# Token lists built by TensorE in SBUF instead of by scatters in DRAM: an attention and mixture-of-experts layer on one core

## What is computed

```python
logits = xt @ gate_w.T
_, idx = top_k(logits + beta, 2)
c = zeros((B, E)).at[arange(B)[:, None], idx].add(sigmoid(logits[idx]))
combined = einsum('beh,be->bh', expert_outputs(xt), c)
shared_out = (silu(xt @ sg) * (xt @ su)) @ sd
return x + attention(xn) + combined + shared_out
```

## Time and profile before

| | us |
|---|---|
| median of 3 runs | 1900.78 (1877.45 to 1905.29) |
| the profiled execution | 1892.56 |
| its span, first to last instruction | 1890.8 |
| mean granted TensorE clock in it | 0.92 |
| PE / DVE / ACT / POOL busy | 89% / 60% / 51% / 51% |
| stage p | 0 to about 330 |
| between p and the first expert matmul | 330 to 348.8 |
| stage c | to about 1050 |
| stage b | to the end |

### The profile page before, as it was taken

One profiled execution on the slowest core, in us unless ns is written; L12 is line 12 of the kernel. 1 busy time (PEld: TensorE's weight loads), 2 busy tenths in 40 slices (PEclk: granted clock), 3 DMA queues, 4 the chain that ended last, 5 costly groups with the idle time before them and its releaser, 6 DMA issues.

```text
span 1890.8 us, 39124 instructions
## 1 busy us (share of the span) xinstructions
PE 1679.5 (89%) x11313; PEld 1347.0 (71%) x11313; DVE 1134.2 (60%) x3793; ACT 963.7 (51%) x1914; POOL 962.1 (51%) x915
## 2 busy tenths in 40 slices
PE   5787776699999999999999789999989999899987
PEld 4565654588888888888888556666666666666666
DVE  5657664466566566666665656666656666556642
ACT  4333432445445445445454355666656665556653
POOL 1434345322221221221220268888888888888886
PEclk9778777799999999999999679999989998889998
DMA  5546645544444444444455367666666666566642
GB/s 180 184 162 222 226 173 201 174 152 153 144 146 153 143 153 147 146 155 148 147 150 118 83 140 160 157 158 158 154 144 134 157 153 143 127 152 151 152 116 74
DMA packets 219824, 287.89 MB, mean 152 GB/s; under 512 B 67193, under 2 KB 133882, under 8 KB 219642
## 3 DMA queue, kind: packets, MB, share of 16 engines
q1 hardware_dynamic: 177226, 210.71, 39.9%
q0 software_dynamic: 17728, 38.30, 8.3%
q10 hardware_dynamic: 24816, 38.28, 5.6%
HBM read 194.92 MB, written 82.31 MB: 147 GB/s over the span
## 4 chain that ended last, share of the span: by engine, by line
PE 56%; issue 11%; POOL 8%; DMA 7%; DVE 6%; ACT 5%; another core or an unknown queue 4%; SPq 2%; ACTq 1%; DVEq 0%; POOLq 0%
PE psum L149 30%; PE psum L757 12%; PE psum L1225 4%; PE psum L1265 3%; DMA plain_arena<-y_d,b_ix 3%; POOL plain_arena L1174 2%; DMA split_arena<-k_d 2%; PE psum L1248 2%; PE psum L849 2%; POOL plain_arena L1149 2%; POOL split_arena L1166 1%; DVE plain_arena L1471 1%; POOL plain_arena L1147 1%; ACT plain_arena L1368 1%
## 5 line engine op out<-in xcount | busy, mean ns | idle before, releaser
L149 PE MATMUL psum<-split_arena 128*128 128x512 f32 (+2 forms) x4560 | 1026.5, 378 | 21.3 <-POOL split_arena L1166 8.5
L149 PEld LDWEIGHTS psum<-split_arena 128*128 128x128 f32 x4560 | 794.9, 202 | 179.3 <-issue 19.1
L1471 DVE CUSTOM_DVE_ANT_0 plain_arena<-psum,mask 128x256 f32<-128x256 f32 (+1 forms) x1024 | 340.0, 386 | 275.5 <-PE psum L1225 265.6
L831 POOL DMA_INDIRECT plain_arena<-xn_d,c_ix x156 | 152.4, 977 | 526.0 <-PE psum L849 479.5
L1368 ACT ACTIVATE plain_arena<-psum 128x512 f32<-128x512 f32 (+1 forms) x512 | 251.3, 543 | 278.4 <-PE psum L1248 249.4
L757 PE MATMUL psum<-split_arena 128*128 128x256 f32 x1872 | 233.8, 285 | 0.0
L757 PEld LDWEIGHTS psum<-split_arena 128*128 128x128 f32 x1872 | 226.9, 192 | 0.1
L360 POOL DMA_INDIRECT order_d<-plain_arena,slot x128 | 124.4, 972 | 198.2 <-DVE slot L618 161.1
L1225 PE MATMUL psum<-split_arena 48*128 48x256 f32 (+1 forms) x1024 | 166.6, 350 | 62.6 <-DMA split_arena<-k_d 32.0
L895 ACT ACTIVATE plain_arena<-psum 128x512 f32<-128x512 f32 x156 | 93.4, 599 | 218.0 <-PE psum L149 211.3
L1225 PEld LDWEIGHTS psum<-split_arena 48*128 48x128 f32 x1024 | 104.1, 201 | 139.6 <-issue 67.9
(11 more groups left out here) (146 smaller groups left out, 1745.1 us busy)
## 6 DMA issues: line engine op xcount, KB each, us to landing
plain_arena<-in_gate_w SPq DMA_DIRECT2D x39, 512.0 KB
plain_arena<-in_up_w SPq DMA_DIRECT2D x39, 512.0 KB
plain_arena<-in_down_w SPq DMA_DIRECT2D x39, 512.0 KB
y_d<-plain_arena ACTq DMA_DIRECT2D x39, 512.0 KB, 2.6
plain_arena<-in_x SPq DMA_DIRECT2D x32, 512.0 KB
q_d<-split_arena SPq DMA_DIRECT2D x32, 512.0 KB
k_d<-split_arena SPq DMA_DIRECT2D x32, 512.0 KB
split_arena<-q_d SPq DMA_DIRECT2D x128, 128.0 KB, 4.0
```

The source lines that it names most:

```text
L149: last = pe.matmul(out, lhs_t(p), rhs(q), start=(begins and c == 0 and k == 0), stop=(ends and c == len(chunks) - 1 and k == 2), skip_grou ...
L831: pool.indirect_dma_start(c_x[:, a, :], None, xn_d, bass.IndirectOffsetOnAxis(c_ix[:, u, a, 0:1], 0)).then_inc(c_ldx, 16)
L1471: last = dve.tensor_tensor_reduce(b_junk[:, 2 * par + i % 2, 0:cols], psum[:, par, at:at + cols], mask[:, 2 * P - cols:2 * P], -1.0, 3e38, ...
```

## The change

The list in DRAM, its blanking, the 128 scatters, the 40 list loads and `c_ix` go. In their place stands a table in SBUF, `order[p, n]`: the row number that belongs to slot 128n + p, for NC = 156 columns. It is a sum over all (row, choice) pairs of an outer product: a row vector that marks partition `slot mod 128`, times a column vector that marks column `slot div 128` and holds the row number.

- POOL, for each batch (2T = 8 pairs of tile and choice): 6 small instructions in a chain that split slot into mod and div, then 24 `tensor_scalar` instructions that write bf16 marks: `in_row` (128 columns), and `in_col` twice (156 columns: the multiple of 128 of the row number, and its remainder).
- PE, at the end of each turn, `tokens_to_slots` of t-2: 16 bf16 matmuls (128 x 128 weights, 156 columns), summed in PSUM bank 1.
- DVE, at the end of each turn, `token_places` of t-2: adds the 156 columns to `order_f`. After the turns one copy to `order`.
- PE's `turn_rows` also waits for `token_places` of an earlier turn (`p_or`), and the value totals move from bank 1 to bank 6.
- POOL's gathers in stage c take their indices from `order`, and wait for no list load; SP's loop in stage c no longer waits for the gather nor loads lists.
- In a block, slot a*128+p now stands at partition p, tile a, so `y_d` is stored in runs of 1 KB in place of 4 KB.

```diff
-            pool.memset(blank, 0).then_inc(s_norow, 1)
+            pool.memset(order_f[:, :], 0.0).then_inc(s_oz, 1)
...
             for b in range(B):
+                v = b % 2
+                flat = slot[:, b * T:(b + 1) * T, :].rearrange("p t k -> p (t k)")
                 pool.wait_ge(p_at, b + 1)
-                for a in range(T):
-                    for c in range(2):
-                        pool.indirect_dma_start(
-                            order_d, bass.IndirectOffsetOnAxis(slot[:, b * T + a, c:c + 1], 0),
-                            token[:, b * T + a, :], None).then_inc(p_sc, 16)
+                if b >= 2:
+                    pool.wait_ge(p_om, b - 1)
+                then = chain(b)
+                then(pool.tensor_copy(slot_at[:, :], flat))
+                then(pool.tensor_scalar(slot_pc[:, 1, :], slot_at[:, :], 1.0 / P, 0.5 * (1 - P) / P, ALU.mult, ALU.add))
+                then(pool.tensor_scalar(slot_pc[:, 1, :], slot_pc[:, 1, :], ROUND, None, ALU.add))
+                then(pool.tensor_scalar(slot_pc[:, 1, :], slot_pc[:, 1, :], -ROUND, None, ALU.add))
+                then(pool.tensor_scalar(slot_pc[:, 0, :], slot_pc[:, 1, :], -float(P), None, ALU.mult))
+                then(pool.tensor_tensor(slot_pc[:, 0, :], slot_pc[:, 0, :], slot_at[:, :], ALU.add))
+                for n in range(2 * T):
+                    pool.tensor_scalar(in_row[:, v, n, :], steps_f[:, 0:P], slot_pc[:, 0, n:n + 1], None, ALU.is_equal)
+                    pool.tensor_scalar(in_col[:, v, 0, n, :], steps_f[:, :], slot_pc[:, 1, n:n + 1],
+                                       float(P * (b * T + n // 2)), ALU.is_equal, ALU.mult)
+                    last = pool.tensor_scalar(in_col[:, v, 1, n, :], steps_f[:, :], slot_pc[:, 1, n:n + 1],
+                                              column[:, 0:1], ALU.is_equal, ALU.mult)
+                last.then_inc(p_oh, 1)
...
                 after(pe, p_rd, b - 2)
+                after(pe, p_or, b - 3)
...
+            def tokens_to_slots(b, v):
+                pe.wait_ge(p_oh, b + 1)
+                after(pe, p_or, b)
+                for n in range(2 * T):
+                    for k in range(2):
+                        last = pe.matmul(psum[:, 1, 0:NC], in_row[:, v, n, :], in_col[:, v, k, n, :],
+                                         start=(n == 0 and k == 0), stop=(n == 2 * T - 1 and k == 1))
+                last.then_inc(p_om, 1)
...
+                if old_b is not None:
+                    tokens_to_slots(old_b, old_u % 2)
...
+            def token_places(b):
+                dve.wait_ge(p_om, b + 1)
+                dve.tensor_tensor(order_f[:, :], psum[:, 1, 0:NC], order_f[:, :], ALU.add).then_inc(p_or, 1)
...
                     allot(done[0])
+                if old[0] is not None:
+                    token_places(old[0])
             dve.sem_inc(p_lo, 2 * KD)
             over_turns(dve, turn)
 
+            dve.wait_ge(p_or, B)
+            dve.tensor_copy(order[:, :], order_f[:, :]).then_inc(p_ord, 1)
...
             weights(0, None)
-            sp.wait_ge(p_sc, 32 * T * B)
-            for u in range(2):
-                order(u, u)
             projected(sp)
...
-                sp.wait_ge(c_ldx, 16 * T * blk + 16 * T)
-                order(blk + 2, u)
...
                 for a in range(T):
-                    pool.indirect_dma_start(c_x[:, a, :], None, xn_d, bass.IndirectOffsetOnAxis(c_ix[:, u, a, 0:1], 0)
+                    pool.indirect_dma_start(c_x[:, a, :], None, xn_d,
+                                            bass.IndirectOffsetOnAxis(order[:, T * blk + a:T * blk + a + 1], 0)
                                             ).then_inc(c_ldx, 16)
...
-                act.dma_start(y_d[ds(blk * BLK, BLK), :].rearrange("(p a) d -> p a d", p=P),
+                act.dma_start(y_d[ds(blk * BLK, BLK), :].rearrange("(a p) d -> p a d", p=P),
```

More of the change, by code:

```diff
@@ L352, in p_gpsimd, with chain, then @@
                                channel_multiplier=1).then_inc(s_const, 1)
-            pool.wait_ge(s_blank, 16)
-            pool.wait_ge(s_iota, 3)
+            pool.wait_ge(s_steps, 1)
+            ROUND = 12582912.0
+            def chain(b):
+                k = [0]
+                def then(ins):
+                    k[0] += 1
+                    ins.then_inc(p_ps, 1)
+                    pool.wait_ge(p_ps, 6 * b + k[0])
+                return then
             for b in range(B):
+                v = b % 2
+                flat = slot[:, b * T:(b + 1) * T, :].rearrange("p t k -> p (t k)")
                 pool.wait_ge(p_at, b + 1)
-                for a in range(T):
-                    for c in range(2):
-                        pool.indirect_dma_start(
-                            order_d, bass.IndirectOffsetOnAxis(slot[:, b * T + a, c:c + 1], 0),
-                            token[:, b * T + a, :], None).then_inc(p_sc, 16)
+                if b >= 2:
[14 more added lines that the diff above has]
+                last.then_inc(p_oh, 1)
         def p_tensor(pe):
@@ L428, in turn @@
                         prefix(done_b)
+                if old_b is not None:
+                    tokens_to_slots(old_b, old_u % 2)
             pe.wait_ge(s_const, 7)
             over_turns(pe, turn)
+            pe.wait_ge(p_vb, T * B)
             for m in range(KD):
                 for c in range(KD):
-                    last = pe.matmul(psum[:, 1, m * B:(m + 1) * B], wvg_raw[:, c, m * P:(m + 1) * P], xsum[:, c, :],
+                    last = pe.matmul(psum[:, 6, m * B:(m + 1) * B], wvg_raw[:, c, m * P:(m + 1) * P], xsum[:, c, :],
                                      start=(c == 0), stop=(c == KD - 1))
@@ L696, in p_vector @@
             for m in range(KD):
[L697 removed]
+                dve.tensor_scalar(vtot[:, :, m], psum[:, 6, m * B:(m + 1) * B], bv_col[:, m:m + 1], ATTN_EPS,
                                   ALU.add, ALU.mult)
@@ L728, in moe_attention_layer @@
         c_ldx = sem("c_rows_gathered")
-        c_il = [sem(f"c_order_loaded{u}") for u in range(2)]
-        c_ix = sb("c_ix", [P, 2, T, 16], U32)
         c_tr = sem("c_transposed")
@@ L826, in c_gpsimd, with gather @@
         def c_gpsimd(pool):
-            def gather(blk, u, n):
-                after(pool, c_tr, blk)
-                hold(pool, c_il[u], 16 * n + 16)
+            def gather(blk):
+                if blk:
+                    pool.wait_ge(c_tr, blk)
                 for a in range(T):
-                    pool.indirect_dma_start(c_x[:, a, :], None, xn_d, bass.IndirectOffsetOnAxis(c_ix[:, u, a, 0:1], 0)
+                    pool.indirect_dma_start(c_x[:, a, :], None, xn_d,
+                                            bass.IndirectOffsetOnAxis(order[:, T * blk + a:T * blk + a + 1], 0)
                                             ).then_inc(c_ldx, 16)
@@ L835, in c_gpsimd @@
                 pool.wait_ge(p_xst[v], 16 * (B // 2))
-            gather(0, 0, 0)
+            pool.wait_ge(p_ord, 1)
+            gather(0)
             pool.wait_ge(s_proj, 4)
             pool.memset(b_k.bitcast(F32), 1.0).then_inc(b_kz, 1)
-            def body(blk, u, n, more):
-                if more:
-                    gather(blk + 1, 1 - u, n + u)
-            over_blocks(pool, body)
+            for blk in range(1, NBLK):
+                gather(blk)
         def c_tensor(pe):
```

37 lines of the change are left out of this document (21 added, 16 removed).

## The result

The changed kernel took 1954.78 us (median of 4 runs, 1941.44 to 1962.14) where the kernel before took 1894.09 (4 runs): a ratio of 1.032 with a 95% interval of 1.024 to 1.040, slower. The forecast was 1856, and 1905 the end of the range. The profiled execution took 1949.99, its span is 1948.2 us.

What follows compares the result with a forecast made beforehand. Stage p was taken as held by scatters delaying PE's signals, stage c by PE. Turns -36, p to c -9, y store +1 sum to -44 against 1892.56: 1848.6; with the median's 8.2 above the profile, 1856, range 1830 to 1905.

Steps and rivals of the forecast that it cites:

- It is one operand in, so I take 8.7.: POOL's marks in stage p, priced by the affine selects: 8.7 us a batch, 13 us if priced by tensor_tensor.
- the turns that were forecast to give 36 us back: Stage p: a turn falls from 19.07 to 16.5 us, over 14 turns with scatters -36 us.
- 24T + 1.2: POOL's burst of marks a batch if one mark takes T us; a turn can't be shorter than it.
- rival 3: Stage p: POOL becomes the bound, slower; 2% lost from about T = 0.83, about 2000 us at 0.97; chance 0.09.
- The scatters hold the turn ... as a delay of PE's signals.: Stage p: PE results due during scatters reach readers only afterwards; without them ACT's 5.07 us and DVE's 5.51 us go.
- PE wants it at the end of its next turn, some 13 us on; both ends fit, the upper one only just.: Stage p: POOL's burst starts at the slots and, at 8.7 to 13 us, is done before PE needs the marks.
- PE's and DVE's additions.: Stage p, each turn: PE's 16 matmuls in tokens_to_slots 2.0 us, DVE's token_places 0.3 us.
- About 15.2: Stage p: DVE's turn of 14.6 us becomes about 15.2 with hand-over gaps, before contention.
- Contention, 1.3 us a turn.: Stage p: POOL's SBUF reads delay DVE's 19 small instructions by 0 to 4.8 us a turn, 1.3 taken.
- From p to c, -9.: From the last slots to the experts: lists ready at 326.1 in place of about 335.5, -9 us, ends -1 and -11.
- Nothing in it [stage c] that the change touches is late.: Stage c is PE's alone, busy 39.63 of 40 us; its 39 blocks were to stay unchanged.
- The y store, +1.: From c to b: the store with 1 KB runs, once on the chain, bounded by 2.65 and 5 us: +1.

Runs made afterwards that it cites:

- e3: Changed kernel without all 24 mark instructions a batch, the rest of the change kept: 1820.65 us, ratio 0.998 to the kernel before.
- e5: Changed kernel with 16 fp32 marks and 8 fp32 products a batch in place of 24 and 16: 1873.08 us, ratio 1.029 to the kernel before.
- e1: Kernel before without its 128 scatters, every slot gathering row 0: 1823.53 us, ratio 0.999 to the kernel before.
- r2_after: Changed kernel, unchanged, measured again on another chip: 1941.50 us, ratio 1.068 to the kernel before.
- e6: Changed kernel with 16 fp32 marks, PE's sum and DVE's addition one batch later, one loop round less: 1849.18 us, ratio 0.974 to the kernel before.
- e7: Changed kernel with fp32 products but without its 16 fp32 marks, tables zero: 1847.09 us, ratio 0.971 to the kernel before.
- r4: Kernel before without its scatters, a third time, on another chip: 1841.28 us in one run, beside 1902.45 for the kernel before.
- r1: Kernel before, unchanged, run for its trace on another chip: 1809.78 us in one run, beside 1822.67 for the kernel before there.
- r3: Kernel before without its 128 scatters, a second time, on another chip: 1824.07 us, ratio 1.000 to the kernel before.
- e4: Kernel before with 40 POOL instructions of several forms behind its end, all other engines idle: 1870.80 us in one run.

## Why the prediction was wrong, point by point

- **"It is one operand in, so I take 8.7."** This is the step that failed, a term mis-sized by a factor of 2.4: the marks take 21.3 us a batch. With that burst over every turn, the turns that were forecast to give 36 us back cost 20.7 + 17.5 = 38 more on F, and the end of p cost 16.5 where -9 was forecast. I priced a `tensor_scalar` by the affine selects because both read one tensor; it goes by 2.5 ns a column, the rate of `tensor_tensor` in the same rows, and a second operation comes on top. The upper end of 13 us had the right rate for one operation and left out the second, and the gaps of up to 0.1 us between marks. By my own rule (24T + 1.2) rival 3 needs T = 0.75 us to exceed the turn of 19.07; the mean mark is (0.606 + 0.814 + 0.881) / 3 = 0.77, and with the gaps and the chain in it the burst of 21.3 is what T = 0.84 gives. The rival came true, with 0.09 on it, just beyond the 0.83 at which it put a loss of 2%; by its own terms, 14 x (21.3 - 19.07) in the turns and -9 + 2 x (21.3 - 8.7) at the end, the loss is 47 us, measured 61.
- **"The scatters hold the turn ... as a delay of PE's signals."** That they cost is shown on C, where taking them away alone gives a turn of 15.00 and 61 us, turns and end of p together; I had taken 36 for the turns. That they cost it as a delay of PE's signals is read from F's trace alone; C has no trace of the kernel before, and F no run without the scatters. On A and B the scatters hold nothing, and there the change had nothing to win in the turns: what it costs is 119 us on B (1941.50 - 1822.67) and 61 on F (1954.78 - 1894.09), and the 58 us between are close to what the scatters cost on C. What the path of that delay is, and what differs between the chips, stays open.
- **"PE wants it at the end of its next turn, some 13 us on; both ends fit, the upper one only just."** Wrong too: in e3 PE is there 9.3 us after the slots. The 8.7 taken would have fitted with some 0.4 us to spare, the upper end of 13 not: with e5's bursts of 13.5 us every other turn waits, up to 3.8 us, and the ratio is 1.029.
- **PE's and DVE's additions.** For PE 2.0 taken, 2.26 measured at a granted clock of 0.50 (after, 214.17 to 216.43, right after PE's wait for the marks), and 1.24 in most turns of e3, where PE doesn't stand still in front of them (clock 1.00 from 150 to 165 us). For DVE 0.3 taken, 0.32 measured. Together with the six small POOL instructions they make the turn 15.39 in place of 15.11 (e3, e1).
- **"About 15.2" for a turn without contention.** The mean of e3 is 15.39, but this is luck: the sum of DVE's parts knew only one kind of turn, and there are ordinary ones of 14.3 and, twice in twelve, long ones of 21.
- **Contention, 1.3 us a turn.** It is there, at about half of that. Groups of the same two instructions in r2_after, with marks, and then in e3_no_marks, both between 60 and 240 us:

```profile
L610 DVE TENSOR_TENSOR plain_arena<-plain_arena,beta_sb 128x32 f32<-128x32 f32 x8 | 2.2, 273 | 1.1 <-DVE part L583 0.2
L580 DVE TENSOR_SCALAR mean<-part 128x4 f32<-128x4 f32 x8 | 1.9, 231 | 0.3
```

```profile
L607 DVE TENSOR_TENSOR plain_arena<-plain_arena,beta_sb 128x32 f32<-128x32 f32 x12 | 2.3, 191 | 1.9 <-DVE part L580 0.7
L577 DVE TENSOR_SCALAR mean<-part 128x4 f32<-128x4 f32 x11 | 1.9, 170 | 0.4
```

  Others keep their lengths (L626 in r2, 217 ns, and its counterpart in e3, 218). The four runs of small instructions of a turn (statistics, choice, root, places), each from the start of its first to the end of its last, take 8.4 us together in e3 and 9.0 in r2, means between 60 and 240 us: +0.6. In the changed kernel POOL's burst is longer than DVE's turn, so this costs nothing. Where DVE's turn counts it may: e6's ordinary turns are 0.5 us longer than e7's, and its small instructions take 9.0 us in place of 8.4. That these belong together is not shown. The rule cited there from the Trainium skill, SBUF — State Buffer, "Who interferes with whom", makes the later of two such instructions wait for the whole of the other; this case doesn't show so much: no small DVE instruction in r2 lasts over 0.41 us, beside marks of 0.60 to 0.94.
- **From p to c, -9.** The path itself is nearly that much shorter: from the last slots to the first transposes it is 31.0 us without scatters (e1, 252.0 to 283.0) and 23.1 without marks and list loads (e3, 263.7 to 286.8). In the changed kernel it is 49.5 (351.3 to 400.8), since POOL has 12.1 us of one burst and all of the last, 21.3, still to do.
- **"Nothing in it [stage c] that the change touches is late."** Wrong on F and C: the blocks take 17.82 us on F and, without scatters in p, 17.79 on C (r4), and 17.55 there with the list in SBUF (e7): 9 to 11 us over 39 blocks. On A and B they take 17.5 with the list loads too (e1, r1, r3). Which part of the change does it on F and C, the list loads that go or the stores in runs of 1 KB, no run separates. A wait that grows with it on C, between 400 and 900 us, is DVE's before its copy of a result, in r4_no_scatters and then in e6_sum_later:

```profile
DVE plain_arena L960 <- PE psum L752: 99.9, 28, 3.7
```

```profile
DVE plain_arena L1007 <- PE psum L810: 85.8, 28, 3.2
```

- **The y store, +1.** Its landing on the chain from c to b went from 2.65 to 2.98 us: +0.3.

The terms without the marks can be added up on C, from the kernel without its scatters (r4) to the fp32 kernel without its marks (e7), in their profiled executions. Until the first transposes of c e7 is 4.7 us later (288.7, 284.0): it starts 2.9 later, twelve turns add 12 x 0.41 = 4.9, the last three 4.7, and the path from the last slots gives back 7.8 (25.3 in place of 33.1). In c it gains 9.3 (666.9 in place of 676.1 over 38 blocks), so it enters b 4.2 us earlier (986.9, 991.1). The marks then add what 16 bursts of 21.3 us of POOL are beyond all this: 116.4 us from e3 on A to r2 on B (286.8 to 403.2), 116.9 from r1 to r2, both on B (286.3), against 119 between the medians there.

## What to carry to other kernels

Price a new instruction by the row that shares its form, not by one that shares the number of its operands; where no row has the form, let the dearest neighbour set the middle of the bound, and see whether the engine's total work still fits the stage. Sum that work over the whole stage as well (16 x 21.3 us against some 300): it is the one bound that no placing of waits can move. A burst that fits a turn must also be done when its reader arrives, 9.3 us after the slots here and not a turn; its reader a turn further behind took an ordinary turn from 16.3 to 14.7 us. Compare turns of one kind, too, before a mean of twelve is called equal. And a gain that rests on a wait by no visible mechanism may belong to the chip, or the hour, that the trace was taken on.

## What the runs showed of the hardware

- POOL's `tensor_scalar` takes about 0.27 us + 2.5 ns a column (e4, other engines idle: 592 ns for 128 columns, 1554 for 512), nearly the same beside busy engines (606 for 128), and 2063 with two operations and two columns on 512; a constant in place of a column saves 0.08 us. A copy with a cast of 512 columns takes 604.
- DVE's small instructions beside POOL's marks: some are longer by 0.06 to 0.1 us in the mean (191 to 273 ns, 170 to 231), 0.6 us a turn in all; none by the length of a mark.
- The kernel before took 1822 to 1826 us in three groups of runs, each on another chip (A, B, D), and 1894 and 1902 in two (F, C; F may be one of the four). In F's trace a result of TensorE that falls due during a run of indirect scatters is seen by ACT 1.62 and 1.63 us after the last of them; in B's it is copied while they run. Without scatters in stage p, that stage turns alike on C and on A (15.00 and 15.11). Whether the chip or something else of the group makes the difference is open.
